# Weights of one expert tile issued earlier, two kinds of items moved between slots, and q's columns put in another order, in a two-layer transformer kernel

## Chip, cores and metric

The kernel runs on one core of one Trainium2 chip. The metric is the device time of one execution in microseconds (us), as the median of several runs. Five engines work on their own queues in program order: TensorE (PE in the profile), VectorE (DVE), ScalarE (ACT), GpSimd (POOL) and SyncE (SP), which here only issues DMAs. They hand work to each other over semaphores.

## What is computed

Input are 8 sequences of 256 tokens with 256 features. Two layers follow each other. Layer 0 is an attention with 16 heads and rotary parts, gated by a feed-forward block. Layer 1, which the change touches, is this:

```python
x = x + attention(xn) * silu(moe(xn))          # xn = layernorm(x)

# attention: 16 heads of 16 features, 256 tokens, 8 batches
q, k, v = split(xn @ w_qkv.T)
q = rmsnorm(q, q_norm_w); k = rmsnorm(k, k_norm_w)      # over the 16 features of a head
out = softmax(q @ k.T * 16 ** -0.5) @ v
out = out @ w_proj.T + b_proj

# moe: top 2 of 8 experts of width 176, and two shared ones
combine = normalised top-2 router probabilities
y = sum_e combine[:, e] * (silu(x @ gate[e]) * (x @ up[e])) @ down[e] + shared(x)
```

## The kernel before, in words

Products are made at high precision from two parts, a high one and a low one: `product` (lines 55 to 60) issues three matmuls, and every tile that feeds one is made in two steps, a copy by ScalarE (high part) and a subtraction by VectorE or GpSimd (low part).

Layer 1 is `stage_layer1`. Its time is cut into slots, `SLOTS` from -16 to 132. A slot n belongs to batch b = n // 16 and position u = n % 16, and in it TensorE makes the scores of head n + 1, then the items of the slot, then the transposes of the probabilities of head n - 1 (`turn`), then the values of head n - 2. There is one bank for scores and one for the transposed tile, so each waits until the other engines have read the one before. VectorE does in its slot the maximum of the scores of head n + 1 (L1699), the low part of the transposed tile of head n - 2 (L1703, named s_wh in the profile), some slot-bound work (the low part of an attention output in slots u = 2, 6, 10, 14, the sums of squares of q in u = 2 and of k in u = 3, the scaling in u = 7 and 8, row statistics in u = 14, the routing in three slots behind the router), then the first half of the slot's items, the reciprocal of the sum of the exponentials (L1730) and the second half of the items. ScalarE makes the exponentials (L1489) and the high parts, GpSimd the normalisation (L1374), the combine multiplication (L1381), the low part of the hidden values (L1385), and three rounds of a reciprocal root in u = 4, 5, 6.

The items of a slot come from `attn_jobs` (line 1095): Q0 and Q1 (projection of q and k for the next batch) at u = 0 and 1, V at 5, T (turn of the normalised rows) at 3, P0 and P1 (output projection of the batch before) at 3 and 4, X0 and X1 at `X_AT`: the turn of q and k of the first and second half of the heads. The router L and the turn of the combine weights C come once in two batches (a step s has 512 tokens). Between them a planner (lines 1117 to 1128) spreads the expert tiles: g, G, u, U are the four pieces of tile K (three matmuls over 512 columns each), D0 and D1 its down projection, taken two tiles later. It adds `SLOT_GOAL - UNIT` = 18.7 of credit a slot, takes off the costs of the items and fills in pieces, so moving an item moves pieces too. `halves` (line 1145) splits the items in two. A tile K belongs to step s = K // 14 with k = K % 14; the first three tiles of a step are the shared experts, the others take combine weights from DRAM.

SyncE's queue (lines 1245 to 1330) issues, tile by tile, the weights of the pieces (`load_gu`, 512 KB), of D (`load_d`, 256 KB), once a step the combine weights to DRAM (`store_combine`, which waits for its landing) and tile by tile back, spread over partitions (`load_cb`). In between, `stack_until` issues what the slots so far ask for: `store_stack` stores a turned half of q and k (X0 or X1) to DRAM, four stores, and `load_stack` loads two pairs of heads of it, four loads of q and one of k. The scores read the stacks.

In DRAM q lies as [half, parity, feature, low, pair, token], since its columns are ordered by `head_columns` as half, feature group, pair; parity is the head's place in its pair. So a load of q has runs of two pairs, and the sum over the 16 features of a head (`sum_squares`, L1625) reads with a step of 4 for q and 8 for k (`q = (4, 8)[r]`).

## Time and profile before

| | us |
|---|---|
| median of 3 runs | 1396.88 |
| lowest and highest | 1396.48, 1396.93 |
| the profiled execution | 1398.46 |
| its span, first to last instruction | 1396.7 |

| engine | busy us | share of the span |
|---|---|---|
| TensorE matmul | 1352.6 | 97% |
| TensorE weight load | 1205.1 | 86% |
| VectorE | 906.8 | 65% |
| ScalarE | 756.2 | 54% |
| GpSimd | 727.8 | 52% |

The profile is of one execution. Its times are those of that execution, with the span counted from the first instruction. Layer 1 begins at about 890 us. The mean granted clock of TensorE is 0.996 of full. Lines (L1699) are lines of the kernel file; names such as l_nb are the tiles' names with a prefix for the stage. In a timeline row, what stands in brackets is how long the engine was idle just before, and what ended that.

### The profile page before, as it was taken

Reading aid. Unit: us, or ns where it says so; the run is one execution under the profiler, and the core shown is the slowest. Engines: PE = TensorE matmul, PEld = TensorE weight load, DVE = VectorE, ACT = ScalarE, POOL = GpSimd, SP = SyncE. Lnnn points to the kernel's source line nnn. Section 1 sums busy time; section 2 is a strip of 40 time slices with the busy share of each in tenths; the row PEclk is TensorE's granted clock in tenths of the full one; section 3 lists DMA queues with packets and bytes.
Section 4 is the critical chain, followed back from the end, with each engine's and each line's share of the span. In section 5 each row is a group of like instructions: output and inputs, shape, how many; then the busy total and the mean of one; then the engine's idle time right before and its main releaser. Section 6 shows DMA issues by size and latency. Waiting matters only on the chain. (4 is left out here: it accounts for less than half of the span.)

```text
span 1396.7 us, 25325 instructions
## 1 busy us (share of the span) xinstructions
PE 1352.6 (97%) x8758; PEld 1205.1 (86%) x8758; DVE 906.8 (65%) x1807; ACT 756.2 (54%) x1964; POOL 727.8 (52%) x719
## 2 busy tenths in 40 slices
PE   8999899999999999999999999889999999999998
PEld 7887798999899989998998898768889888888897
DVE  6655566566656665666565665557887778786765
ACT  4553454445544555455545444246666666666664
POOL 1651343445343555344635453447657676766775
PEclk9999999999999999999999999999999999999999
DMA  5995333224422353234324424266555663645662
GB/s 185 318 337 202 84 91 97 84 77 120 113 82 49 103 144 85 62 91 114 97 63 120 118 63 127 95 189 186 162 169 156 197 176 112 205 138 181 177 194 91
DMA packets 105646, 190.51 MB, mean 136 GB/s; under 512 B 20433, under 2 KB 39569, under 8 KB 103217
## 3 DMA queue, kind: packets, MB, share of 16 engines
q1 hardware_dynamic: 105520, 188.91, 45.5%
q8 instruction: 71, 1.16, 0.4%
q14 instruction: 55, 0.44, 0.1%
HBM read 116.41 MB, written 30.47 MB: 105 GB/s over the span
## 5 line engine op out<-in xcount | busy, mean ns | idle before, releaser
L776 POOL TENSOR_TENSOR a_pr<-a_pr,a_ri 128x512 f32<-128x512 f32 x128 | 133.4, 1042 | 299.9 <-DVE a_ri L956 299.9
L833 ACT ACTIVATE a_pr<-a_score,a_nb 128x256 f32<-128x256 f32 x256 | 119.2, 471 | 267.7 <-DVE a_nb L948 267.7
L1374 POOL TENSOR_TENSOR l_pr<-l_pr,l_ri 128x512 f32<-128x512 f32 x128 | 133.3, 1042 | 126.4 <-DVE l_ri L1730 125.2
L1489 ACT ACTIVATE l_pr<-l_score,l_nb 128x256 f32<-128x256 f32 x256 | 119.3, 472 | 100.7 <-DVE l_nb L1699 100.7
L58 PE MATMUL a_job<-s_xs,s_wh 128*128 128x512 f32 x384 | 153.6, 400 | 1.0 <-PEq L222 1.0
L60 PE MATMUL a_job<-s_xs,s_wl 128*128 128x512 f32 x384 | 152.1, 396 | 0.0
L59 PE MATMUL a_job<-s_xs,s_wh 128*128 128x512 f32 x384 | 151.4, 394 | 0.0
L948 DVE TENSOR_REDUCE a_nb<-a_score 128x2 f32<-128x512 f32 x128 | 88.5, 692 | 86.1 <-PE a_score L1027 84.2
L1699 DVE TENSOR_REDUCE l_nb<-l_score 128x2 f32<-128x512 f32 x128 | 87.5, 684 | 32.1 <-PE l_score L1838 31.9
L961 DVE TENSOR_TENSOR a_pt<-a_turn,a_pt 128x512 fp32r<-128x512 f32 x128 | 87.5, 684 | 23.8 <-ACT a_pt L841 23.8
L58 PE MATMUL l_job<-l_xs,s_wl 128*128 128x512 f32 x224 | 90.3, 403 | 5.9 <-DMA s_wl<-wgu_scratch 5.8
L1497 ACT ACTIVATE s_wh<-l_turn 128x512 fp32r<-128x512 f32 x128 | 76.8, 600 | 35.4 <-PE l_turn L1848 35.4
L1703 DVE TENSOR_TENSOR s_wh<-l_turn,s_wh 128x512 fp32r<-128x512 f32 x128 | 87.3, 682 | 8.6 <-ACT s_wh L1497 8.2
L1862 PE MATMUL l_out<-s_wh,l_vp 128*128 128x256 f32 x512 | 91.9, 301 | 0.2 <-DVE s_wh L1703 0.2
L60 PE MATMUL l_job<-l_xs,s_wl 128*128 128x512 f32 x224 | 89.5, 399 | 0.0
L59 PE MATMUL l_job<-l_xs,s_wl 128*128 128x512 f32 x224 | 89.2, 398 | 0.0
L1848 PE MATMUL l_turn<-s_ident,l_pr 128*128 128x128 f32 x512 | 78.0, 275 | 11.3 <-DVE s_wh L1703 10.2
L956 DVE RECIPROCAL a_ri<-a_sm 128x2 f32<-128x2 f32 x128 | 21.3, 166 | 102.3 <-ACT a_pr L833 102.3
L60 PEld LDWEIGHTS a_job<-s_xs,s_wl 128*128 128x128 f32 x384 | 72.1, 188 | 16.8
L1848 PEld LDWEIGHTS l_turn<-s_ident,l_pr 128*128 128x128 f32 x512 | 58.7, 140 | 29.1 <-issue 12.8
L58 PEld LDWEIGHTS a_job<-s_xs,s_wh 128*128 128x128 f32 x384 | 72.3, 188 | 11.3 <-issue 1.4
L59 PEld LDWEIGHTS a_job<-s_xs,s_wh 128*128 128x128 f32 x384 | 72.3, 188 | 10.5
(252 smaller groups left out, 4565.4 us busy)
## 6 DMA issues: line engine op xcount, KB each, us to landing
s_wl<-wgu_scratch SPq DMA_DIRECT2D x56, 512.0 KB, 5.7
a_sk<-a_rotk SPq DMA_DIRECT2D x384, 64.0 KB, 2.0
a_sq<-a_rotq SPq DMA_DIRECT2D x256, 64.0 KB, 2.0
s_xs<-xn_scratch SPq DMA_DIRECT2D x14, 1024.0 KB, 5.6
l_wd<-wd_scratch SPq DMA_DIRECT2D x56, 256.0 KB, 2.9
l_zq<-qs_scratch SPq DMA_DIRECT2D x128, 64.0 KB, 4.3
l_sk<-ks_scratch SPq DMA_DIRECT2D x32, 256.0 KB, 4.7
a_raw<-in_w SPq DMA_DIRECT2D x30, 256.0 KB, 2.9
```

Source lines behind the costliest of these rows:

```text
L58: pe.matmul(out, lh, rh, start=first, stop=False)
L59: pe.matmul(out, lh, rl, start=False, stop=False)
L60: return pe.matmul(out, ll, rh, start=False, stop=last)
L776: pool.tensor_tensor(e, e, ri[:, n % 2, :].unsqueeze(2).broadcast_to([P, 2, SEQ]), ALU.mult)\
L833: i = act.activation(pr[:, n % 2, t, :], PS[n % 2][:, t * SEQ:(t + 1) * SEQ], ACT.Exp, bias=nb[:, n % 2, t:t + 1], accum_out=sm[:, n % 2, ...
L948: dve.tensor_reduce(nb[:, (n + 1) % 2, :], PS[(n + 1) % 2][:, :].rearrange("p (t k) -> p t k", t=2), AX.X, ALU.max, negate=True).then_inc( ...
L961: dve.tensor_tensor(pt[:, n % 2, 1, :], PT[:, :], pt[:, n % 2, 0, :], ALU.subtract).then_inc(S["turn_free"], 1)
L1374: pool.tensor_tensor(e, e, ri[:, n % 3, :].unsqueeze(2).broadcast_to([P, 2, SEQ]), ALU.mult)\
L1489: i = act.activation(pr[:, n % 3, t, :], PS[n % NPS][:, t * SEQ:(t + 1) * SEQ], ACT.Exp, bias=nb[:, n % 3, t:t + 1], accum_out=sm[:, n % 3 ...
L1699: dve.tensor_reduce(nb[:, (n + 1) % 3, :], PS[(n + 1) % NPS][:, :].rearrange("p (t k) -> p t k", t=2), AX.X, ALU.max, negate=True).then_in ...
L1848: i = pe.transpose(PT[:, kc * SEQ + t * P:kc * SEQ + (t + 1) * P], pr[:, n % 3, t, kc * P:(kc + 1) * P], ident[:, :])
L1862: i = pe.matmul(PO[:, 0:SEQ], vp[:, kc, a, e * P:(e + 1) * P], pt[:, n % 2, q, kc * SEQ:(kc + 1) * SEQ], start=(e == 0 and kc == 0 and q = ...
```

## The change

- `X_AT`: X1 of batches 1 to 7 comes in slot 13 instead of 10. X0, and batch 0, stay.
- P0 and P1 come in slots 4 and 5 instead of 3 and 4, but for the last batch's, which stay in slots 131 and 132.
- Only in step 0, `load_gu` of tile 5 (K = 4 is `first_combine`) is issued in front of the stack loads and the combine store asked for at K = 4, instead of at the start of K = 5.
- q's columns are ordered half, parity, pair, feature. The sum of squares of q reads with a step of 1; the scaling likewise. The DRAM copy is [half, parity, pair, feature, low, token], the stores and the four q loads of a stack follow, each partition now in two runs of 256 values instead of one of 512. `norm_w` is ordered for both. k's own order is as before.

The planner's result for three places, from working its sums through (items of a slot):

```
slot  before                          after
10    X1 D0 u U                       D0 u U D1
13    D1 g G                          X1 g G
19    T P0                            T D0 u
20    P1 l L                          U P0 l L
21    V                               V P1
22    D0 u                            (empty)
23    U D1 g                          D1 g
28    g G D0                          G D0 u
29    u U D1                          U X1 D1
35    T P0                            T g G
36    P1 g                            P0 D0
37    G V                             V P1
```

```diff
     def X_AT(m):
-        return (8, 9) if m == 0 else (9, 10)
+        return (8, 9) if m == 0 else (9, 13)
...
-        if u in (3, 4) and b >= 1:
-            jobs.append((f"P{u - 3}", b - 1))
+        first = 3 if b == BATCH else 4
+        if u in (first, first + 1) and b >= 1:
+            jobs.append((f"P{u - first}", b - 1))
...
-                        sp.dma_start(qs_dram[m % 2, half, :, :, low].rearrange("h d p n -> (h d) p n"), tqk[:, half, 0, low, :].bitcast(F32))                           .then_inc(tqk_out[half], 16)
+                        sp.dma_start(qs_dram[m % 2, half, :, :, :, low].rearrange("h p d n -> (h p d) n"), tqk[:, half, 0, low, :].bitcast(F32))                           .then_inc(tqk_out[half], 16)
...
-                        own = qs_dram[m % 2, half, h, :, :, j:j + PER_LOAD].rearrange("d c p n -> (d c) (p n)")
+                        own = qs_dram[m % 2, half, h, j:j + PER_LOAD].rearrange("p d c n -> (d c) p n")
                         for base in (64 * h, 64 * h + 32):
-                            sp.dma_start(zq[base:base + 32, h, at, :].bitcast(F32).rearrange("k p n -> k (p n)"), own)                               .then_inc(zq_in[stack_of(i)], 16)
+                            sp.dma_start(zq[base:base + 32, h, at, :].bitcast(F32), own)                               .then_inc(zq_in[stack_of(i)], 16)
...
                 for K in range(L + 1):
-                    if 2 <= K < L:
+                    s, k = step_of(K)
+                    first_combine = k == NSH + 1 and s == 0
+                    if 2 <= K < L and not (k == NSH + 2 and s == 0):
                         stack_until(AT["U", K - NGU] if K >= NGU else SLOTS[0])
                         load_gu(K)
                     if K >= 1:
                         stack_until(AT["D1", K - 1 - ND] if K > ND else SLOTS[0])
                         load_d(K - 1)
-                    s, k = step_of(K)
+                    if first_combine:
+                        load_gu(K + 1)
                     if k == NSH + 1 and s < NSTEP:
                         stack_until(AT["C", s])
                         store_combine(s)
...
                 def sum_squares(m, r):
-                    q = (4, 8)[r]
+                    q = (1, 8)[r]
...
                 def scale_rows(m, r):
-                    q = (4, 8)[r]
+                    q = (1, 8)[r]
...
-    qs = nc.dram_tensor("qs_scratch", [2, 2, 2, D1, 2, 4, SEQ], F32, kind="Internal").ap()
+    qs = nc.dram_tensor("qs_scratch", [2, 2, 2, 4, D1, 2, SEQ], F32, kind="Internal").ap()
...
-    return np.concatenate([q.transpose(0, 2, 3, 1, 4).reshape(D, D), k.transpose(0, 3, 1, 2, 4).reshape(D, D), w[2 * D:]])
+    return np.concatenate([q.transpose(0, 2, 1, 3, 4).reshape(D, D), k.transpose(0, 3, 1, 2, 4).reshape(D, D), w[2 * D:]])
...
-        "norm_w": _np.stack([_np.tile(_np.repeat(i[f"L1_attn_{s}_norm_w"], 4), 2) for s in "qk"], axis=1),
+        "norm_w": _np.stack([_np.tile(i[f"L1_attn_{s}_norm_w"], 8) for s in "qk"], axis=1),
```

## Rows read from the trace of the kernel before

**Rows 1.** Windows: stretch, length, busy us of each engine, clock, DMA share, GB/s.

```profile
400.00:700.00 300.00, 300.00 (x1950) 269.67 (x1949) 184.75 (x325) 154.67 (x395) 139.85 (x108) 1.00 0.34 95
...
1100.00:1200.00 100.00, 96.16 (x666) 86.48 (x665) 80.20 (x187) 68.77 (x198) 67.78 (x92) 1.00 0.53 158
```

**Rows 2.** Table of waits, TensorE, layer 1: in total, times, longest.

```profile
PE l_turn L1848 <- DVE s_wh L1703: 10.2, 26, 1.0
```

**Rows 3.** Timeline of TensorE, slot 115, which holds P0 and g: start, duration.

```profile
1338.13 0.40 PE L1838 MATMUL l_score<-l_sk,l_zq 128*128 128x256 f32 x2
1338.37 0.28 PE L58 MATMUL l_job<-s_wl,l_ot 128*128 128x256 f32 x1
...
1339.79 0.39 PE L58 MATMUL l_job<-l_xs,s_wl 128*128 128x512 f32 x1
...
1340.48 0.60 PE L1848 MATMUL l_turn<-s_ident,l_pr 128*128 128x128 f32 x4
...
1341.39 0.40 PE L1838 MATMUL l_score<-l_sk,l_zq 128*128 128x256 f32 x2
```

**Rows 4.** Timeline of TensorE: the scores with which slots 20, 21, 22 begin.

```profile
1002.96 0.40 PE L1838 MATMUL l_score<-l_sk,l_zq 128*128 128x256 f32 x2
...
1007.29 0.40 PE L1838 MATMUL l_score<-l_sk,l_zq 128*128 128x256 f32 x2
...
1010.09 0.39 PE L1838 MATMUL l_score<-l_sk,l_zq 128*128 128x256 f32 x2
```

**Rows 5.** Timeline, slot 42: scores, VectorE's maximum, the next scores.

```profile
1080.44 0.40 PE L1838 MATMUL l_score<-l_sk,l_zq 128*128 128x256 f32 x2
...
1082.49 0.68 DVE L1699 TENSOR_REDUCE l_nb<-l_score 128x2 f32<-128x512 f32 x1
...
1084.85 0.39 PE L1838 MATMUL l_score<-l_sk,l_zq 128*128 128x256 f32 x2
```

**Rows 6.** Timeline of TensorE: slot -1's g5, scores of slots 0 and 126.

```profile
931.25 0.77 PE L58 MATMUL l_job<-l_xs,s_wl 128*128 128x512 f32 x1 [5.80 <-DMA s_wl<-wgu_scratch]
...
935.23 0.63 PE L1838 MATMUL l_score<-l_sk,l_zq 128*128 128x256 f32 x2
...
1374.67 0.40 PE L1838 MATMUL l_score<-l_sk,l_zq 128*128 128x256 f32 x2
```

**Rows 7.** Windows, columns as in rows 1: the stretch behind the stall.

```profile
930.00:935.00 5.00, 3.75 (x11) 3.21 (x12) 0.18 (x1) 2.36 (x7) 3.99 (x6) 0.50 1.06 302
```

**Rows 8.** Timeline of GpSimd around the stall.

```profile
929.52 1.26 POOL L1381 TENSOR_TENSOR l_ga<-l_ga,l_cb 128x512 f32<-128x512 f32 x1 [10.15 <-DMA l_cb<-ct_scratch]
931.52 1.28 POOL L1385 TENSOR_TENSOR l_hid<-l_ga,l_hid 128x512 fp32r<-128x512 f32 x1 [0.74 <-ACT l_hid L1512]
```

**Rows 9.** Timeline of SyncE's queue: combine store, combine load, weights of tile 5.

```profile
922.27 0.54 SPq L1259 DMA_DIRECT2D ct_scratch<-l_ct  x1
924.54 0.36 SPq L1268 DMA_DIRECT2D l_cb<-ct_scratch  x1
924.94 0.43 SPq L1248 DMA_DIRECT2D s_wl<-wgu_scratch  x1
```

**Rows 10.** DMA issues of 256 KB of combine weights; q loads and q stores, ns on SyncE.

```profile
l_cb<-ct_scratch SPq DMA_DIRECT2D x16, 256.0 KB, 4.2
...
L1289 SPq DMA_DIRECT2D l_zq<-qs_scratch x128: 332/422/2137, 919.8 to 1352.2; - x128
...
L1274 SPq DMA_DIRECT2D qs_scratch<-l_tqk x32: 517/602/650, 914.0 to 1312.2; - x32
```

**Rows 11.** Instructions of L1625, eight for q and eight for k: ns min/median/max.

```profile
L1625 DVE TENSOR_REDUCE l_ss<-l_sqr x16: 1048/1104/1172, 899.2 to 1283.1; 128x32 f32<-128x512 f32 x16
```

**Rows 12.** Groups of instructions from 890 us: the maximum of the scores.

```profile
L1699 DVE TENSOR_REDUCE l_nb<-l_score 128x2 f32<-128x512 f32 x128 | 87.5, 684 | 32.1 <-PE l_score L1838 31.9
```

**Rows 13.** Timeline of VectorE, slot 41: the low part of X0.

```profile
1080.33 0.49 DVE L1577 SCALAR_TENSOR_TENSOR l_tqk<-l_job,s_nqk,l_tqk 128x256 fp32r<-128x256 f32 x1 [1.13 <-ACT l_tqk L1461]
```

**Rows 14.** Timeline of TensorE, slot 28: D0 of tile 14.

```profile
1034.47 0.36 PE L1758 MATMUL l_down<-l_wd,l_hid 128*128 128x256 f32 x1 [0.69 <-DVE l_y L1681]
```

## The prediction

> **What bounds the kernel now.** The page's first part gives the first reading: TensorE is busy for 97% of the span, VectorE for 65%. The windows of layer 0 show TensorE full from 400 to 700 us and nearly so before; nothing of the change lies there, so its time stays. In layer 1 TensorE is busy for 96 us of 100 [rows 1]. There the table of waits is read next: from 925 us on TensorE waits 26 times, 10.2 us in all, in its transposes of the probabilities on VectorE [rows 2], once for 5.8 us on the weights of tile 5, and twice on the bias sum of a finished step.
>
> The timeline of one full slot gives the prices of TensorE's work [rows 3]: from start to start the scores take 0.24 us, a projection (12 products) 1.42, a piece of an expert tile 0.69, transposes and values 0.91. A slot without items is thus 1.15 us of work; D0 or D1 is 0.71 (six products of 0.118), Q and V cost as much as P, T, X and C 0.35 each, and the router 1.76 (slot 20, with P1, lasts 4.33 [rows 4]). With W as a slot's sum, a slot that nothing holds up lasts W: this one holds 1.15 + 1.42 + 0.69 = 3.26 and lasts 3.26.
>
> The timeline of slot 42 shows what holds one up [rows 5]. Its scores start at 1080.44, but VectorE, late from slot 41, takes their maximum at 1082.49: a lag of 2.05. Then come its low part of the turned tile, the transposes that wait for it, values, and the next scores at 1084.85, which is 2.36 us behind the maximum. So a slot lasts max(W, lag + 2.36), and an entirely empty one, with the smallest lag of 0.43, 2.79: slot 21, W 2.57, lasts 1010.09 - 1007.29 = 2.80 with a lag of 0.43 [rows 4]. I read the lag of all 127 slots this way from the same two timelines; the rule gives the length within 0.03 us in over twenty of the held-up ones. From slot 0 to the end of slot 125 (935.23 to 1374.67 us [rows 6]) 439.4 us pass and the W sum to 414.8. These 24.6 us, and the stall before slot 0, are all that a new order of the same work can win.
>
> **Early weights.** The stall looks like 5.8 us plus a half clock: TensorE stops at 925.4, resumes at 931.25 [rows 6], and from 930 to 935 the granted clock is 0.50, its 1.2 GHz level, at which half of the time is lost [rows 7]; it is back at 936.2. With g5 and G5 at the slow pace that is some 8 us. But behind G5 in slot -1 stands D0 of tile 3, and it needs that tile's hidden values, which are late themselves: GpSimd waited 10.15 us for the combine weights, multiplied at 929.52, ScalarE copied, and GpSimd subtracted at 931.52 for 1.28 us [rows 8]. So D0 could start at 932.80 at the soonest against 933.95, where it started. And that chain hangs on SP's queue: eight stores of the turned halves from 914.02 on, wd, the first stack, then the combine store at 922.27, its landing, and the combine load at 924.54; the weights of tile 5 are issued behind it, at 924.94 [rows 9]. The change puts them (0.43 us of SP) in front of the stack, the combine store and the load. Combine load, then D0, move later by 0.43, and by up to four times 0.18 more if the q loads, which become three-dimensional, take SP as long as the stores do (0.60 for 0.42 us). The load's 4.8 us to landing may fall to 4.2, the median for its size, without 512 KB right behind it [rows 10]. D0 then starts at 932.6 to 933.95, TensorE having stood still since some 927. At half pace it takes 1.28 us, so the next scores start at 933.9 to 935.2 against 935.23: 0 to 1.3 us won. The clock came back 5 us after TensorE resumed; if it does so again, it is back at 937.6 or later where it was back at 936.2, and slots 0 and 1 have 2.7 us more of slow time, half of it lost: 1.35. Net between 1.35 lost and 0.05 lost; up to 3.4 won (2.9 on the scores and the 0.5 that slot 0 lost to the slow clock) if the shorter stop does not drop the clock. I take 0.3 lost: slots 0 and 1 hang in part on VectorE, which the slow clock does not touch. Stack 0 gets 512 KB ahead of it and may hold the first scores for up to 1 us, which the later wait for D0 hides.
>
> **q by parity, pair, feature.** The sum of squares of q reads with a step of 4 values, that of k of 8: the 16 of them take 1.05 to 1.17 us, those of q the lower end [rows 11]. Step 1 is nearest to the maximum over 512 values, 0.684 [rows 12]. So 0 to 0.38 us of VectorE a batch; I take 0.38, in slot 2 of each batch, so the lag at slot 3 is smaller. The scaling makes the same 512 results. The q loads fetch two runs of 1 KB for one of 2 KB in each partition; the stores write 1 KB runs already, and in all of layer 1 the scores waited once, for 0.2 us, on a stack: nothing, up to 1 us lost.
>
> The Trainium skill, "SBUF — State Buffer", "Door 1: The DMA port swizzle", has 16-byte lines and calls a step of 4 fp32 free. By it the new order wins nothing and the sum is 2.0 us longer; the 1.05 us beside 0.684 speaks against that, though the second reads PSUM, so it is rival (e).
>
> **Second half's turn at slot 13.** Nothing goes; X1 moves. A slot with an X costs VectorE 1.13 us of waiting for ScalarE's two copies [rows 13] and 0.8 of its own, 4.0 to 4.6 us in all for W 2.9, so the next begins with a lag of 1.5 to 2.05 and lasts 0.6 to 1.2 over W. In the kernel before the second X follows at once and drags the lag over slots 10 to 12. After the change slot 10 has time to catch up, and slot 14 pays a second time. The planner's sum, worked through with the new items, puts four pieces in some slots 10, 11 and 12. Over W in slots 9 to 16, before and after by the rule: batch 0 1.5 and 1.0; 2 2.5 and 2.9; 3 0.6 and 0.4; 4 2.1 and 1.8; 5 1.9 and 0.65; 6 2.8 and 2.5. Batch 1 has 3.2 and 3.6: there X1 meets the gate of step 0 (two operations over 512 values) in slot 29, and D0 of tile 14 comes behind one piece where it came behind two, so its 0.69 us wait for the bias sum [rows 14] becomes 1.4. Sum 14.6 to 12.85: 1.75 us won. Bounds: if each X slot costs as slot 41 did, 2 lost; if ScalarE is free sooner in slot 13, 5 won. SP issues the four stores of X1 four slots later; the stack that needs them is asked for only in slot 4 of the next batch, so this costs nothing; it would if that queue ran three slots late.
>
> **Projections in slots 4 and 5.** Batches 1, 3 and 5 (slots 20, 52, 84) have the router there. The planner now fills slot 19 with a D0 and a piece, slot 20 with U, P0 and the router (W 5.0), slot 21 with V and P1 (3.99), and leaves slot 22 empty. The empty slot still lasts 2.79: 1.6 over W, and slot 23, W 2.54, another 0.45 since the routing on VectorE leaves a lag of 0.63. Before, slots 19 to 23 were 1.24, 1.29 and 1.50 over W; after 2.1 each. In batches 2, 4 and 6 P0 leaves the slot with the second sum of squares and the xs split, but G comes there: 0.72, 0.9, 0.5 before, 0.86, 1.05, 0.45 after. Batch 0 wins 0.4 from the shorter sum alone. Sum 6.6 to 8.7: 2.1 us lost, with the 0.38s of q inside. Bounds: 5 lost if GpSimd (three rounds of the root, a spread and a normalise in slots 20 to 22) is late too; 1 won if the lags are as small as in batch 7. The last projections stay in slots 131 and 132, and the end is unchanged.
>
> **The sum.** -0.3 + 1.75 - 2.1 = -0.65 won, so 0.6 us longer: a span of 1396.7 becomes 1397.3, and the profiled execution's 1398.46 becomes 1399.1. It lies 1.6 above the median of the three runs, 1396.88, so against that I forecast 1397.5.
>
> **Rivals.**
> (a) No change within 0.2% (2.8 us, about what a measurement of this kernel can tell from none), as summed: 0.41.
> (b) Clock kept and lags small: the stop before slot 0 is short enough for the full clock, 3.4 won, and slots 9 to 16 win 3 while slots 22, 54 and 86 cost 1.5 in all: 1396.9 - 4.9 = 1392. For it: TensorE would stand still for some 5 us instead of 5.8. Against: in those 5.8 us the level fell [rows 7]. Chance 0.27.
> (c) The weights were all of the stall, because the combine load lands far sooner without them behind it: D0 at 932 or before, 4.5 to 8 won, 1390. Against: 256 KB of combine weights take 4.2 us as the median, too. Chance 0.04.
> (d) Slower by the empty slots 22, 54 and 86. It decides from the point where slots 19 to 21 give nothing back: 1.64 + 0.44 each, 6.2 in all, and X1 beside the row statistics of slot 14 loses the 2 of its bound, while the shorter sums win 3.5: 4.7 longer, 1401.6. Chance 0.2.
> (e) The order of q does not do what it says: the sum stays at 1.05 us. Slot 3 then starts with a lag 0.38 larger and lasts some 0.29 longer in seven batches: 2.0, so 1399.5. Chance 0.08.
> Faster by over 0.2% are (b) and (c), 0.31; the same (a) and nearly all of (e), 0.48; slower (d) and the rest, 0.21. The range 1391 to 1401.5 leaves out half of (c) and of (d); for the likeliest alone it is 1394.5 to 1399.6.
>
> **What would show it.** L1625 for q at 0.69; the wait on the weights gone and TensorE waiting some 5 us on GpSimd's hidden values in slot -1 in its place; the combine load issued at 925 or later; slots 22, 54 and 86 lasting 2.8; a 1.4 us wait on the bias sum in slot 28; lags of 1.5 to 2 at slots 10 and 14. I am wrong if D0 of tile 3 starts before 932, if the clock stays full through 930 to 940, or if slot 14 begins with a lag below 1.

## The result, and the profile after

The changed kernel takes 1399.9 us (median of 20 runs, 1397.52 to 1402.98), the kernel before 1397.43 (median of 20, 1395.72 to 1402.71). The ratio is 1.0018, with a 95% interval from 1.0011 to 1.0024: 2.5 us slower, inside the 0.2% that I had called no change, and four times the 0.6 us of my sum. The profiled execution of the changed kernel has a span of 1399.9 us and a time of 1401.74.

The page of the changed kernel, first the busy time of each engine, then the transfers, then two groups of instructions and one of DMA issues:

```profile
PE 1353.7 (97%) x8758; PEld 1208.1 (86%) x8758; DVE 908.7 (65%) x1807; ACT 757.3 (54%) x1964; POOL 725.0 (52%) x719
...
DMA packets 109741, 190.51 MB, mean 136 GB/s; under 512 B 20432, under 2 KB 47760, under 8 KB 107312
...
L1703 DVE TENSOR_REDUCE l_nb<-l_score 128x2 f32<-128x512 f32 x128 | 87.6, 684 | 39.0 <-PE l_score L1842 38.5
...
L1852 PE MATMUL l_turn<-s_ident,l_pr 128*128 128x128 f32 x512 | 77.9, 274 | 15.5 <-DVE s_wh L1707 15.2
...
l_zq<-qs_scratch SPq DMA_DIRECT2D x128, 64.0 KB, 4.6
```

The engines' lines of layer 1 stand 4 further down than in the kernel before, SyncE's 1. The row that matters is that of the transposes of the probabilities: TensorE waited 10.2 us there before [rows 2] and waits 15.2 now. VectorE itself has longer pauses for want of scores, 39.0 us where it had 32.1 [rows 12]. The two engines' busy time grows by only 1.1 and 1.9 us; they wait for each other more often. The loads of q, now in two runs a partition, land after 4.6 us in the median (4.3 before), and TensorE never waits for one in layer 1 of this execution.

I split the span by the instants at which slots begin (the scores in TensorE's timeline), and take each slot's own work off its length, by the prices of the prediction:

| part, profiled executions, us | before | after | difference |
|---|---|---|---|
| start of the span to the first TensorE instruction of layer 1 | 891.80 | 894.20 | +2.40 |
| from there to the scores of slot 0 | 43.43 | 41.35 | -2.08 |
| slots 0 to 125 | 439.44 | 442.43 | +2.99 |
| scores of slot 126 to the end of VectorE's last instruction | 19.40 | 19.39 | 0 |
| over W: slots 0 to 2 of the batches | 1.72 | 2.03 | +0.31 |
| slots 3 to 7 | 7.25 | 12.20 | +4.95 |
| slot 8 | 1.82 | 1.24 | -0.58 |
| slots 9 to 16 | 14.53 | 12.78 | -1.75 |

Slot 16 of a batch is slot 0 of the next, so it stands in two rows (0.72 us before, 0.66 after); slots 9 to 15 alone are 13.81 and 12.12.

The 2.40 us of the first row are none of the change: its code for layer 0 is the same, and over the kernels below this stretch lasts 889.4 to 893.5 us with no relation to what they change. Part of it can be seen. In this execution TensorE waited 2.79 us for a load at 142 us, and its granted clock then fell to 1.2 GHz for part of the window from 145 us, and once more in that from 165 us, so that its mean in both is 0.66 of full; in the execution of the kernel before it is 1.00 in both. Windows with their columns as in [rows 1]:

```profile
145.00:150.00 5.00, 5.00 (x21) 4.30 (x21) 1.00 (x3) 1.62 (x5) 1.04 (x1) 0.66 0.43 105
...
165.00:170.00 5.00, 4.31 (x17) 3.81 (x18) 2.63 (x5) 1.86 (x6) 0.73 (x2) 0.66 0.38 90
```

Of the fourteen executions only e9_x_by_batch also has such stretches in layer 0, and these two begin layer 1 last, at 894.20 and 893.53. Layer 1 itself became 0.91 us longer in this pair of executions.

**Before slot 0.** The timelines of TensorE (first row), GpSimd (two) and SyncE's queue (three), and the windows with their columns as in [rows 1]:

```profile
934.11 0.58 PE L1762 MATMUL l_down<-l_wd,l_hid 128*128 128x256 f32 x1 [4.48 <-POOL l_hid L1389]
...
930.79 1.26 POOL L1385 TENSOR_TENSOR l_ga<-l_ga,l_cb 128x512 f32<-128x512 f32 x1 [9.01 <-DMA l_cb<-ct_scratch]
932.79 1.27 POOL L1389 TENSOR_TENSOR l_hid<-l_ga,l_hid 128x512 fp32r<-128x512 f32 x1 [0.74 <-ACT l_hid L1516]
...
921.65 0.45 SPq L1249 DMA_DIRECT2D s_wl<-wgu_scratch  x1
924.64 0.54 SPq L1260 DMA_DIRECT2D ct_scratch<-l_ct  x1
927.28 0.35 SPq L1269 DMA_DIRECT2D l_cb<-ct_scratch  x1
...
930.00:935.00 5.00, 0.89 (x4) 0.89 (x5) 0.76 (x2) 2.03 (x6) 3.48 (x3) 0.90 0.97 303
935.00:937.00 2.00, 2.00 (x9) 1.81 (x9) 0.78 (x2) 0.69 (x2) 2.00 (x5) 0.50 1.04 297
```

The weights are issued three microseconds ahead of the combine store, and the 5.80 us wait for them [rows 6] is gone. In its place D0 of tile 3 waits 4.48 us for its hidden values, and the chain behind that is the one of [rows 8, 9], one for one: GpSimd waits 9.01 us for the combine weights, multiplies, ScalarE copies, GpSimd subtracts. One thing differs from what I had: the combine load lands 3.51 us after its issue (927.28 to GpSimd's start at 930.79), where it took 4.98 before. And the clock falls to 1.2 GHz only from 934.0 and is full again at 937.4, 3.3 us after TensorE resumed; before, it was down from 929.5 to 936.3, until 5 us after TensorE resumed.

**Slots 21 to 23**, one of the three places where the planner leaves a slot empty. TensorE's timeline:

```profile
1011.90 0.39 PE L1842 MATMUL l_score<-l_sk,l_zq 128*128 128x256 f32 x2
1013.80 0.63 PE L1852 MATMUL l_turn<-s_ident,l_pr 128*128 128x128 f32 x4 [1.51 <-DVE s_wh L1707]
1014.74 0.40 PE L1842 MATMUL l_score<-l_sk,l_zq 128*128 128x256 f32 x2
1017.18 0.63 PE L1852 MATMUL l_turn<-s_ident,l_pr 128*128 128x128 f32 x4 [0.64 <-DVE s_wh L1707]
1018.12 0.39 PE L1842 MATMUL l_score<-l_sk,l_zq 128*128 128x256 f32 x2
```

The empty slot 22 lasts 2.84 us for 1.15 of work, with a wait of 1.51; slot 23 lasts 3.38 for 2.54. Slots 54 and 55 last 3.04 and 3.38, slots 86 and 87 2.90 and 3.38. VectorE (five rows) and GpSimd (two) over the same time:

```profile
1007.80 1.12 DVE L1598 TENSOR_TENSOR l_lg<-l_lg,l_m 128x32 f32<-128x32 f32 x1
...
1012.38 0.68 DVE L1703 TENSOR_REDUCE l_nb<-l_score 128x2 f32<-128x512 f32 x1
...
1014.11 0.49 DVE L1663 TENSOR_TENSOR l_eq<-l_eq,l_m 128x32 f32<-128x32 f32 x1
...
1015.33 0.32 DVE L1667 TENSOR_TENSOR l_oh<-l_oh 128x32 f32<-128x32 f32 x1
...
1015.77 0.67 DVE L1703 TENSOR_REDUCE l_nb<-l_score 128x2 f32<-128x512 f32 x1
...
1007.57 1.30 POOL L1385 TENSOR_TENSOR l_ga<-l_ga,l_cb 128x512 f32<-128x512 f32 x1
...
1013.28 1.27 POOL L1389 TENSOR_TENSOR l_hid<-l_ga,l_hid 128x512 fp32r<-128x512 f32 x1
```

From maximum to maximum VectorE's slot 22 takes 3.39 us; I had its routing at the length that it had before (2.99), which would have made the lag at slot 23 0.63. It is 1.03. The instruction at 1014.11 has only 32 values a partition, yet it ends when GpSimd's subtraction over 512 ends (1014.60 and 1014.55), and the one at 1007.80 ends with GpSimd's multiplication (1008.92 and 1008.87). In the kernel before, the same two, in VectorE's timeline:

```profile
1007.16 0.59 DVE L1594 TENSOR_TENSOR l_lg<-l_lg,l_m 128x32 f32<-128x32 f32 x1
...
1012.66 0.24 DVE L1659 TENSOR_TENSOR l_eq<-l_eq,l_m 128x32 f32<-128x32 f32 x1
```

Here the moved pieces of the expert tiles bring GpSimd's long operations beside the routing. The long one, at 1007.80, costs TensorE nothing, since slot 21 has 3.99 us of work of its own; the quarter of a microsecond at 1014.11 and the 0.12 at 1015.33 (0.32 us for 0.20) stand in the slot that has nothing to hide them, and are most of the 0.40.

The other traces bear this out. Over all fourteen, 34 of the routing's VectorE instructions with two inputs in SBUF began within a GpSimd operation of over 1 us that had at least 0.25 us to go: every one ended 0.04 to 0.06 us behind it and took 0.42 to 1.15 us. The 43 beside one that have a single SBUF input (the copy, the reductions, the addition from the matmul's bank l_job) took 0.17 to 0.19. The 60 instructions of the three routings of slots 0 to 125 take 12.25 us before, 11.9 to 12.3 in the kernels below that leave the projections of the router's batches in slots 3 and 4, 15.65 in the changed kernel, 15.64 in e10 and e12 and 14.37 in e1; the time by which the overlapped ones exceed 0.19 us makes 0.40 us of it before and 3.39 after. The Trainium skill, "SBUF — State Buffer", "SBUF: two separate sides", has VectorE operations with two SBUF inputs and GpSimd's share one pair of ports that one of them holds for a whole instruction; these ends agree with it. No kernel here takes the overlap away alone.

**q's order.** VectorE's sixteen sums of squares, min/median/max in ns:

```profile
L1629 DVE TENSOR_REDUCE l_ss<-l_sqr x16: 671/872/1167, 901.5 to 1285.5; 128x32 f32<-128x512 f32 x16
```

Against 1048/1104/1172 before [rows 11]. The eight of q take 0.67 to 0.68 us (0.68 at 901.54), the eight of k 1.07 to 1.17 (1.11 to 1.17 before).

### The profile page after: what moved, and what is told of

It is laid out like the page before. It is cut to its first block and busy times, and to the rows that moved or that the text cites. A ratio compares the mean times of both kernels' runs of the same rounds, so it can differ in the third digit from the quotient of the medians.

```text
span 1399.9 us, 25325 instructions
## 1 busy us (share of the span) xinstructions
PE 1353.7 (97%) x8758; PEld 1208.1 (86%) x8758; DVE 908.7 (65%) x1807; ACT 757.3 (54%) x1964; POOL 725.0 (52%) x719
## 5 line engine op out<-in xcount | busy, mean ns | idle before, releaser
L1852 PE MATMUL l_turn<-s_ident,l_pr 128*128 128x128 f32 x512 | 77.9, 274 | 15.5 <-DVE s_wh L1707 15.2
```

The costliest lines, as they stand in the source:

```text
L1852: i = pe.transpose(PT[:, kc * SEQ + t * P:kc * SEQ + (t + 1) * P], pr[:, n % 3, t, kc * P:(kc + 1) * P], ident[:, :])
```

## The experiments

Twelve kernels, each timed against the kernel before on its own chip; there the kernel before had medians of 1398.11 us (e1 to e4), 1397.18 (e5 to e8) and 1396.67 (e9 to e12), so it is the ratios that compare. "Slots" is the length of slots 0 to 125 in the profiled execution, "to slot 3" the time from layer 1's first TensorE instruction to the scores of slot 3 (it takes in the stall and the slow clock behind it), "turn" TensorE's wait for VectorE in the transposes from the page:

| kernel | ratio, 95% interval | median, us | to slot 3 | slots | turn |
|---|---|---|---|---|---|
| before | 1 | 1397.43 | 52.47 | 439.44 | 10.2 |
| after | 1.0018, 1.0011 to 1.0024 | 1399.90 | 50.80 | 442.43 | 15.2 |
| e1_p_only | 1.0042, 1.0030 to 1.0054 | 1404.06 | 52.26 | 446.59 | 18.2 |
| e2_x_only | 0.9979, 0.9968 to 0.9990 | 1395.10 | 51.45 | 437.25 | 7.3 |
| e3_weights_only | 0.9993, 0.9985 to 1.0002 | 1396.80 | 51.15 | 441.01 | 10.2 |
| e4_q_only | 0.9973, 0.9963 to 0.9983 | 1394.26 | 51.77 | 437.03 | 7.5 |
| e5_no_p | 0.9960, 0.9946 to 0.9975 | 1391.58 | 51.35 | 436.46 | 7.5 |
| e6_p_even | 0.9978, 0.9967 to 0.9989 | 1394.34 | 53.72 | 437.38 | 9.9 |
| e7_store_first | 0.9948, 0.9932 to 0.9964 | 1390.43 | 50.86 | 436.65 | 7.5 |
| e8_best | 0.9938, 0.9922 to 0.9953 | 1388.76 | 48.87 | 436.26 | 7.3 |
| e9_x_by_batch | 0.9962, 0.9947 to 0.9976 | 1392.48 | 51.83 | 436.61 | 6.8 |
| e10_after_store_first | 0.9991, 0.9982 to 1.0000 | 1396.09 | 48.82 | 442.55 | 14.8 |
| e11_q_and_x | 0.9958, 0.9944 to 0.9973 | 1391.60 | 51.08 | 435.03 | 7.7 |
| e12_p_odd | 0.9999, 0.9989 to 1.0009 | 1396.51 | 51.07 | 440.83 | 13.1 |

A difference between two kernels is taken between the ratios, 0.001 being 1.4 us, and has an error of some 2 us; where the timelines say the same, I trust it more. The timelines are of one execution each. How well their sums repeat is seen in e3, whose edit ends before slot 0: its slots are 1.57 us longer, 0.33 of it in slot 0 and the rest in slots 14 to 95. Slot 70 alone takes part in many of these differences, since TensorE waits at its end up to 1.1 us for a stack in some executions (0.16 before, 1.09 in e5) and not at all in others (the changed kernel).

### The four parts alone

The kernel before with the projections' move alone:

```diff
-        if u in (3, 4) and b >= 1:
-            jobs.append((f"P{u - 3}", b - 1))
+        first = 3 if b == BATCH else 4
+        if u in (first, first + 1) and b >= 1:
+            jobs.append((f"P{u - first}", b - 1))
```

> The kernel before with P0 and P1 in slots 4 and 5 alone. Theory S (slots): the cost of this edit in the changed kernel was 4.9 us in slots 3 to 7 of the batches (7.25 us over W before, 12.2 after), and here the sum of squares of q is not shorter, so 5 to 6.5 us longer than before; slots 22, 54 and 86, empty, last 2.8 to 3.3 and slots 23, 55, 87 3.4 (W 2.55). Theory E (elsewhere): what the changed kernel lost does not sit in these slots but was there already at the start of layer 1, which came 2.4 us later in its profiled execution; then this kernel is within 1.5 us of before.

Measured: 5.9 us slower, within theory S's bounds, and theory E falls. Slots 3 to 7 of the batches are 13.27 us over W where they were 7.25, the three pairs of empty slots and their successors last 2.87/3.38, 2.80/3.32 and 2.83/3.39, and TensorE's wait in the transposes is the largest of all kernels. The group of the page:

```profile
L1849 PE MATMUL l_turn<-s_ident,l_pr 128*128 128x128 f32 x512 | 78.1, 275 | 18.3 <-DVE s_wh L1704 18.2
```

The second half's turn at slot 13 alone:

```diff
-        return (8, 9) if m == 0 else (9, 10)
+        return (8, 9) if m == 0 else (9, 13)
```

> The kernel before with X1 in slot 13 alone. Theory S: slots 9 to 16 of all batches were 14.5 us over W before and 12.8 after the whole change, slot 8 of batch 4 another 0.5 less: 1.7 to 2.2 us faster than before, batch 5 winning most (1.45) and batch 2 losing 0.7. Theory E: no part of it is worth more than 1 us, the time is that of before within 1 us.

Measured: 3.0 us faster, above the expectation, whose value the interval (1.4 to 4.5 us) holds. The slots are 2.19 shorter, and the wait in the transposes falls from 10.2 to 7.3. Theory E falls.

The early weights alone:

```diff
-                    if 2 <= K < L:
+                    s, k = step_of(K)
+                    first_combine = k == NSH + 1 and s == 0
+                    if 2 <= K < L and not (k == NSH + 2 and s == 0):
...
-                    s, k = step_of(K)
+                    if first_combine:
+                        load_gu(K + 1)
```

> The kernel before with the weights of tile 5 issued ahead of the first stack alone. Theory S: from the first instruction of layer 1 on TensorE to the scores of slot 0 took 43.4 us before and 41.4 after, and slot 0 was 0.4 longer: 1.5 to 2 us faster; TensorE waits 4 to 5 us for GpSimd's hidden values in front of D0 of tile 3, and the combine load lands 3.5 us after its issue, since no 512 KB are queued right behind it (4.8 before). Rival theory: those 3.5 us were chance and it lands after 4.8 here too; then D0 starts as late as before and nothing is won (0 to 0.5).

Measured: 1.0 us faster by the ratio, with no change inside the interval: less than theory S's 1.5 to 2, though its steps hold. TensorE's D0, GpSimd's multiplication and the issue of the combine load in the three timelines:

```profile
930.61 0.58 PE L1761 MATMUL l_down<-l_wd,l_hid 128*128 128x256 f32 x1 [4.54 <-POOL l_hid L1388]
...
927.29 1.26 POOL L1384 TENSOR_TENSOR l_ga<-l_ga,l_cb 128x512 f32<-128x512 f32 x1 [9.40 <-DMA l_cb<-ct_scratch]
...
923.83 0.35 SPq L1268 DMA_DIRECT2D l_cb<-ct_scratch  x1
```

Again the load is there after 3.46 us. So the shorter landing is no accident of one execution; with the weights right behind the load it takes 4.4 to 5.0 (before, e1, e2, e4, e11), with them in front 3.5 to 3.6 (after, e3, e5, e9, e12), with one execution at 4.6 (e6). The three kernels with the store first, below, have the weights in front too and land at 3.9 to 5.2, so the weights' place is not all of it.

The order of q alone (the same lines as in the change):

```diff
-                    q = (4, 8)[r]
+                    q = (1, 8)[r]
```

> The kernel before with q's columns by parity, pair, feature alone. Theory S: the sum of squares of q falls from 1.06 to 0.68 us in each batch, slot 3 starts with a lag 0.38 smaller where it is not waiting for ScalarE, and lasts up to 0.3 less in six batches: 0.5 to 2 us faster. Theory E: the two runs of 1 KB in place of one of 2 KB in each partition, or the place of the data in DRAM, cost time somewhere: 1 to 2.5 us slower.

Measured: 3.8 us faster, twice the upper end of what was expected; theory E falls. The slots are 2.41 shorter, at the lower end of what the ratio's interval allows (2.4 to 5.2); the rest of the 3.8 is not in them and may be the spread of the medians. With X1 at slot 13 in both kernels the order gives nearly the same in the slots (2.22, e11 against e2), and so does X1 with the new order in both (2.00, e11 against e4). The sixteen sums of squares are 14.5 us in all instead of 17.6, which is 8 times 0.38.

### Without the projections' move, and where its loss lies

The changed kernel with P0 and P1 back in slots 3 and 4:

```diff
-        first = 3 if b == BATCH else 4
-        if u in (first, first + 1) and b >= 1:
-            jobs.append((f"P{u - first}", b - 1))
+        if u in (3, 4) and b >= 1:
+            jobs.append((f"P{u - 3}", b - 1))
```

> The changed kernel with P0 and P1 back in slots 3 and 4. Theory S (the prices of the slots add up): the changed kernel is 2.5 us slower than before and the projections cost it 4.9, so this one is 2 to 3.5 us faster than before. Theory E (the loss is not in these slots): it stays 1.5 to 2.5 us slower than before.

Measured: 0.9960, faster than the kernel before by 5.6 us and than the changed one by 0.58% or some 8 us, of which 5.97 stand in the slots. More than theory S's 2 to 3.5; theory E falls. Its row of the transposes:

```profile
L1851 PE MATMUL l_turn<-s_ident,l_pr 128*128 128x128 f32 x512 | 77.7, 274 | 8.2 <-DVE s_wh L1706 7.5
```

The move in the batches without the router, and then in those with it (the last batch has neither loss nor gain, 0.02 and 0.03 us over W):

```diff
-        first = 3 if b == BATCH else 4
+        first = 4 if b % 2 == 0 and b < BATCH else 3
```

> The changed kernel with P0 and P1 back in slots 3 and 4 in batches 1, 3, 5 and 7 alone; in 2, 4 and 6 they stay in 4 and 5. Theory S: the empty slots beside the router are the loss, 4.2 us of 4.9 in batches 1, 3 and 5; without them this kernel is 1.2 to 2.5 us faster than before. Rival: the projection itself is badly placed in slots 4 and 5 wherever it stands (the G beside the second sum of squares); then only some 2 of the 4.9 come back and this kernel is about as fast as before.

Measured: 0.9978, 3.1 us faster than before, more than theory S's 1.2 to 2.5; the rival, no gain over before, falls. Against e5_no_p the slots are only 0.92 longer, but this execution's D0 waited 5.86 us before slot 0, where others with early weights waited 4.5 to 5.0. Its granted clock was at 1.2 GHz from 899.7 to 906.6 us, where it did not fall in e5_no_p, and the combine store behind that came 2.0 us later after layer 1's start (32.1 against 30.1). So most of its 2.5 us over e5_no_p is not shown to be the projections'.

```diff
-        first = 3 if b == BATCH else 4
+        first = 4 if b % 2 == 1 and b < BATCH else 3
```

> The changed kernel with P0 and P1 in slots 4 and 5 only in batches 1, 3, 5 and 7 (the router's batches and the last), the complement of e6_p_even. Theory R (the empty slots 22, 54 and 86 are most of the loss): slots 3 to 7 at 10.5 to 11.5 us over W, of which batches 1, 3 and 5 some 2.7 each, and 4.0 to 5.5 us over e5_no_p: ratio 0.999 to 1.000. Rival A (both kinds of batch cost alike): 2.5 to 3 us over e5, ratio 0.998. By TensorE's slots alone, which give the even batches only 0.9, it is R with 4.5 us: 0.9992.

Measured: 0.9999, theory R. It costs 0.39% or 5.4 us over e5_no_p, 4.37 of them in the slots; batches 1, 3 and 5 are 2.59, 2.80 and 2.64 us over W in slots 3 to 7 (0.99, 1.11 and 1.23 in e5_no_p), the others as without the move. The group of the page:

```profile
L1852 PE MATMUL l_turn<-s_ident,l_pr 128*128 128x128 f32 x512 | 77.7, 274 | 13.2 <-DVE s_wh L1707 13.1
```

In the slots the two sets of batches make 4.4 and 0.9 of the 5.97; the 0.7 that is left is within what such sums vary by.

### The early weights beside the others

The changed kernel with neither the projections' move nor the early weights (only the lines of q and of slot 13):

```diff
-                    if 2 <= K < L and not (k == NSH + 2 and s == 0):
+                    if 2 <= K < L:
...
-                    if first_combine:
-                        load_gu(K + 1)
```

> The order of q and X1 at slot 13, without the early weights and without the move of the projections. Theory W (the early weights are worth 1 to 2 us beside the others too): 1 to 2 us over e5_no_p, a ratio of 0.9967 to 0.9975, slot 0 reached 42.3 to 43.0 us after layer 1's start, the combine load landing 4.4 to 5.0 us after its issue. Rival Z (the landing time was chance): 0.996 as e5, slot 0 at 41.1, landing at 3.5.

Measured: 0.9958 against the 0.9960 of e5_no_p. Of theory W the mechanism holds (slot 0 is reached after 42.03 us instead of 41.11, the load lands in 4.43) and the price does not: nothing is left of it. Where it goes is seen in slot 0. TensorE's timeline and windows of 1 us of e5_no_p, with early weights:

```profile
929.97 0.58 PE L1761 MATMUL l_down<-l_wd,l_hid 128*128 128x256 f32 x1 [4.79 <-POOL l_hid L1388]
...
931.42 0.63 PE L1841 MATMUL l_score<-l_sk,l_zq 128*128 128x256 f32 x2
...
935.67 0.40 PE L1841 MATMUL l_score<-l_sk,l_zq 128*128 128x256 f32 x2
...
931.42:932.42 1.00, 1.00 (x5) 0.90 (x5) 0.34 (x1) 0.39 (x1) 1.00 (x3) 0.50 1.05 252
...
934.42:935.42 1.00, 1.00 (x4) 0.81 (x3) 0.90 (x5) 0.78 (x2) 0.12 (x1) 0.50 0.83 187
935.42:936.42 1.00, 1.00 (x7) 0.83 (x6) 0.70 (x3) 0.31 (x1) 0.54 (x1) 0.89 0.14 45
```

and of e11_q_and_x, without them:

```profile
929.00 0.77 PE L58 MATMUL l_job<-l_xs,s_wl 128*128 128x512 f32 x1 [4.74 <-DMA s_wl<-wgu_scratch]
...
932.97 0.63 PE L1838 MATMUL l_score<-l_sk,l_zq 128*128 128x256 f32 x2
...
935.60 0.39 PE L1838 MATMUL l_score<-l_sk,l_zq 128*128 128x256 f32 x2
...
932.97:933.97 1.00, 1.00 (x5) 0.92 (x5) 0.69 (x3) 0.08 (x1) 0.90 (x2) 0.67 1.02 290
```

In e5_no_p all of slot 0 runs at 1.2 GHz: 4.25 us from scores to scores, and the clock is back 5.7 us after TensorE resumed. In e11_q_and_x TensorE resumed earlier, with slot -1's g5, G5 and D0 still ahead of it (3.97 us at the slow clock), the clock is back 4.6 us after it resumed, and most of slot 0 is at full speed: 2.63 us. The 0.92 us won ahead of slot 0 are lost in it, and 0.7 more. But this is a reading of two executions, and the slow stretch is not the same from one to the next. In the windows of the fourteen, the clock fell at the stop before slot 0 in all but e8; in three (after, e3, e10) it was down half as long as in the ten others, partly while TensorE still stood, and it was full again 3.2 to 6.2 us after TensorE resumed. The changed kernel has the same early weights and gives back only 0.37 us in slot 0 (3.18 against 2.81). That nothing is left of the weights' gain rests on the medians, with their error of some 2 us.

### The combine store ahead of the queue

e5_no_p with the first combine store ahead of wd and of the stack, its landing awaited behind the stack:

```diff
+                    if first_combine:
+                        stack_until(AT["D1", K - 1 - ND])
+                        wait_free(sp, ("C", 0))
+                        sp.dma_start(ct_dram[0], ct[:, :]).then_inc(ct_stored[0], 16)
                     if K >= 1:
                         stack_until(AT["D1", K - 1 - ND] if K > ND else SLOTS[0])
                         load_d(K - 1)
                     if first_combine:
                         load_gu(K + 1)
-                    if k == NSH + 1 and s < NSTEP:
+                        stack_until(AT["C", s])
+                        sp.wait_ge(ct_stored[0], 16)
+                    elif k == NSH + 1 and s < NSTEP:
```

> The changed kernel without the move of the projections, and with the first combine store issued in front of wd of tile 3 and of stack 0, its landing awaited behind the stack. Theory S (SP's queue sets the stall): the combine load is issued some 2.2 us sooner than in the changed kernel, TensorE waits 2 to 2.5 us instead of 4.5 in slot -1, the clock stays full, and the kernel is 2 to 3 us faster than the one without the move of the projections, 4 to 6 faster than before. Rival: the hidden values of tile 3 come as late as before for another reason (the load lands later for the traffic of the stack in front of it); then it is within 0.7 us of the kernel without the move.

Measured: 0.9948, 1.7 us under e5_no_p by the ratio (1.2 by the medians), a little under what was expected. GpSimd's multiplication and SyncE's issue of the combine load:

```profile
925.43 1.26 POOL L1390 TENSOR_TENSOR l_ga<-l_ga,l_cb 128x512 f32<-128x512 f32 x1 [8.36 <-DMA l_cb<-ct_scratch]
...
920.28 0.59 SPq L1268 DMA_DIRECT2D l_cb<-ct_scratch  x1
```

Both the theory and the rival are right in part. Counted from layer 1's start, the load is issued 2.3 us sooner than in e5_no_p, but it lands 5.15 us after its issue where it took 3.58, so D0 comes only 0.75 us sooner. The stop (TensorE's wait for the hidden values in front of D0) is 3.52 us and not 2 to 2.5, and the clock does fall: TensorE resumed at 928.75 and had the slow clock until 934.96, another 6.2 us, so slot 0 lasts 4.27 us again.

The same on top of the whole change:

> The changed kernel, all four parts, with the first combine store ahead of wd and the stack. Theory S: the store wins what it won in e7 (1.2 us of the median), the stall in slot -1 is 3.5 instead of 4.5 us, slots 3 to 7 are still 12 to 13 us over W: ratio 1.0009, span some 1 us under that of the changed kernel. Rival H (the projections' loss is really a loss of the stall, so a cure of the stall cures it): slots 3 to 7 fall with it, ratio under 0.998.

Measured: 0.9991, 3.8 us under the changed kernel. TensorE's D0, GpSimd's multiplication, and SyncE's store and load:

```profile
927.29 0.39 PE L1768 MATMUL l_down<-l_wd,l_hid 128*128 128x256 f32 x1 [2.75 <-POOL l_hid L1395]
...
923.96 1.28 POOL L1391 TENSOR_TENSOR l_ga<-l_ga,l_cb 128x512 f32<-128x512 f32 x1 [7.36 <-DMA l_cb<-ct_scratch]
...
915.86 0.54 SPq L1327 DMA_DIRECT2D ct_scratch<-l_ct  x1
...
919.79 0.59 SPq L1269 DMA_DIRECT2D l_cb<-ct_scratch  x1
```

The gain is more than theory S's 1.2 us, and its steps hold: the stop shrinks to 2.75 us, slot 3 is reached 2.0 us sooner than in the changed kernel, and slots 3 to 7 stay at 12.44 over W, so the projections' loss is theirs and rival H falls. The group of the transposes has hardly moved:

```profile
L1858 PE MATMUL l_turn<-s_ident,l_pr 128*128 128x128 f32 x512 | 77.8, 274 | 15.0 <-DVE s_wh L1713 14.8
```

The store is also all that sets e8_best below apart from e9_x_by_batch. The three pairs (e7 against e5, e10 against after, e8 against e9) put its worth at 1.7, 3.8 and 3.4 us by the ratios, and at 0.5, 2.0 and 3.0 by the time to slot 3: more than the weights gave in all but the first of the timelines, and spread as the load's landing is (5.15, 4.17 and 3.87 us).

### Slot 13 by batch, and the best version

e7_store_first with X1 at slot 10 again for m of 2, 3 and 4, which are the batches 1 to 3 in which the changed kernel was not shorter in slots 9 to 16:

```diff
-        return (8, 9) if m == 0 else (9, 13)
+        return (8, 9) if m == 0 else (9, 10) if m in (2, 3, 4) else (9, 13)
```

> The kernel with the first combine store in front, and X1 in slot 13 only for batches 1, 5, 6 and 7, in slot 10 for 2, 3 and 4. Theory S: by the slots, X1 at 13 lost 0.7, 0.2 and 0.1 us in those three batches; so 0.5 to 1 us faster than with X1 at 13 in all batches. Rival: the batches influence each other through the lag at their borders and nothing is won or some tenths are lost.

Measured: 0.9938, interval 0.9922 to 0.9953: the fastest of all, 8.4 us under the kernel before on its chip. But its slots are only 0.39 us shorter than e7_store_first's. The rest lies before slot 3 (48.87 against 50.86). D0 waits 2.31 us, and this is the one execution whose clock does not fall behind that stop; TensorE's timeline and one window behind it:

```profile
928.33 0.38 PE L1767 MATMUL l_down<-l_wd,l_hid 128*128 128x256 f32 x1 [2.31 <-POOL l_hid L1394]
...
928.00:929.00 1.00, 0.67 (x5) 0.67 (x6) 0.62 (x2) 0.33 (x1) 1.00 (x2) 1.00 1.05 281
```

Even so the full clock gives little in slots 0 and 1: they last 2.33 and 4.43 us, since TensorE then waits 1.50 us for ScalarE's exponentials, against 4.27 and 2.90 in e7.

The choice by batch on e5_no_p, without the early store, tells the two apart:

> The changed kernel without the move of the projections (e5_no_p), and X1 at slot 13 only for batches 1, 5, 6 and 7's halves, at slot 10 for those of 2, 3 and 4. e8_best beat e7_store_first by 1.7 us of the median with this same edit, but its trace shows only 0.4 us less in slots 0 to 125 and 1.6 less in the stall before slot 0. Theory B (the choice itself matters): 0.4 to 1.0 us under e5_no_p, that is a ratio of 0.9953 to 0.9957 against e5's 0.996, slots 9 to 15 at 11.0 to 11.5 us over W. Rival N (e8's lead was the stall's own variation from execution to execution): 0.996 again, and stalls before slot 0 that differ by up to 1.5 us between kernels that issue the same instructions there.

Measured: 0.9962 to e5_no_p's 0.9960, slots 436.61 to 436.46. Theory B falls: the choice by batch is worth nothing that the slots show, and rival N stands. In the profiled pair e8's lead over e7 is the stretch before slot 0, where both issue the same instructions and the combine load landed after 3.87 us instead of 5.15. That their six runs each differ by 1.7 us in the median for the same reason is argued from this pair and not shown. e7_store_first is as good a version as can be shown, 0.5% faster than the kernel before; e8_best has the lowest median.

## Why the prediction came out as it did

The forecast was no change within 0.2%, 0.6 us longer by the sum and 1397.5 us against the three runs shown. Measured: 1399.9, 2.5 us longer, in the range. The sign of the sum was right and its size a quarter of the measured one. That it came so near is partly luck, since two terms were off in opposite ways: in the pair of profiles the projections cost 2.85 us more than their term, and the stretch up to slot 3, put at 0.3 lost, won 1.67.

**Bound and rule.** TensorE's slots and the lag of VectorE were the right view: what grew between the two pages is the transposes' wait. With the lags of the trace after, the rule max(W, lag + 2.36) gives 4.06 for slot 36 (lag 1.70; it lasts 4.07), 4.59 for slot 42 (lag 2.23; 4.60) and 4.42 for slot 100 (lag 2.06; 4.43). The empty slots begin with lags of 0.48, 0.68 and 0.54, not the least lag of 0.43, and last what the rule makes of that: 2.84, 3.04 and 2.90. Of the 43 slots of the kernel before that VectorE holds up, the rule gives 38 within 0.03 us.

**Early weights: -0.3, the steps right, their balance wrong.** D0 follows GpSimd's hidden values, with a wait of 4.48 us that I had at some 5. D0 came 2.24 us sooner counted from layer 1's start, more than the 1.35 I allowed: the combine load landed in 3.5 us, where I had 4.2 to 4.8, and the q loads took SyncE no longer, 1.84 us for four. In the profiled execution 1.67 us are won by slot 3. But over all kernels, those with the early weights reach slot 3 after 51.24 us on average (five, without e6_p_even; 51.65 with it) and those without after 51.81 (five): 0.2 to 0.6 won, and by the ratios 1.0 alone and none beside q and slot 13. So the price that I put on the clock, 1.35 us given back in slots 0 and 1, is there in some executions (slot 0 at 4.25 in e5 against 2.63 in e11) and small in others (3.18 in the changed kernel against 2.81 before); I was wrong in letting it outweigh the gain. One of the three signs of being wrong did come: D0 before 932. It stands at 934.11 only because layer 0 took 2.40 us longer; counted from layer 1's start it is where 931.7 was in the kernel before. And the 3.4 us that a kept clock was to win do not come out of the prediction's own rows: D0 at 932.6 and 0.64 us for it put the scores at 933.2, 2.0 sooner, which with slot 0's 0.5 is 2.5.

**q's order: right, and perhaps too small.** L1629 is 0.68 for q, as taken; rival (e) falls. I put some 2 us on it. The slots gave 2.4 alone (e4 against before) and 2.2 beside slot 13 (e11 against e2); the ratios say 3.8 and 2.9. By place it came otherwise: I had 0.29 us in slot 3 of seven batches, and in e4 slot 3 is shorter by 0.15 us or more in batches 1, 2 and 6 only, and slot 4 in 2, 4 and 5. By the rule of the Trainium skill, "SBUF — State Buffer", "Door 1: The DMA port swizzle", that a step of 4 fp32 is free, nothing would have been won: the measured 1.05 against 0.68 us decides against it.

**Second half's turn: right in the sum.** 1.75 forecast and 1.75 measured in slots 9 to 16 of the pair (14.53 to 12.78), with lags of 1.68 and 1.50 at slots 10 and 14 of batch 0. Batch by batch it holds less well: batch 1, put at 0.4 lost, lost 0.1, batch 2, put at 0.4 lost, lost 0.7, and batches 0 and 5 won more than forecast. A second sign of being wrong came here: slot 14 begins with a lag below 1 in batches 3, 4 and 5 (0.93, 0.80, 0.54), so the turn in slot 13 does not delay VectorE everywhere as slot 41 had it. The bias sum's wait for D0 of tile 14 became 1.37, forecast 1.4, in TensorE's timeline:

```profile
1035.23 0.35 PE L1762 MATMUL l_down<-l_wd,l_hid 128*128 128x256 f32 x1 [1.37 <-DVE l_y L1685]
```

Alone (e2) it gave 3.0 us.

**Projections: the step that was mis-sized.** "Sum 6.6 to 8.7: 2.1 us lost" was 7.25 to 12.20, 4.95 lost, in the pair; taken apart from q, 4.1 had been forecast (the 2.1 and q's 2.0) and 5.9 to 7.2 in the slots, 6 to 8 by the ratios, was measured (e1 against before, after against e5, e10 against e7). By place: batches 1, 3 and 5, forecast 2.1 each, are 2.59, 2.80 and 2.66. Two thirds of the excess is in slots 23, 55 and 87, which are 0.83 over W where I had 0.45. That was the step "since the routing on VectorE leaves a lag of 0.63"; it is 1.03. I carried over the length the routing had, without asking what GpSimd does beside it after the pieces have moved. Another 0.4 us in all is the empty slots' own lag. Batch 6, forecast 0.45, is 2.07. Of this 0.92 is slot 103's wait for the bias sum, which is there before as well (0.91) and which I left out of both sums: the batch had 1.34 before, not 0.5. The other 1.15 is slot 100, in which VectorE is late from slot 99, where its operation for G waits 0.62 us for ScalarE's tanh (a lag of 2.06, 4.43 us long for 3.28); this I did not work out. Batch 0 was to win 0.4 from the shorter sum and won nothing, because VectorE then waited 0.40 us for ScalarE instead. In batch 2 the forecast holds (0.86; 0.90), in batch 4 it was too high (1.05; 0.62). The lower bound that I gave, 5 lost "if GpSimd is late too", was the nearest to it.

**The rivals.** (b) does not happen in this change: the clock fell all the same. It is real, though, in e8_best, with a stop of 2.31 us. (c) had its true half in the landing time, worth a microsecond and not four. (d) is the one that came nearest in its mechanism, with the empty slots and their successors as its place, at 7.8 us over W for its 6.2; its other half, X1 losing 2 us, is refuted by e2.

**What stays open.** The parts alone sum to 0.13% faster by their ratios, the whole is 0.18% slower. By the slots they sum to 4.1 us longer (7.15 - 2.19 + 1.57 - 2.41) and the whole is 2.99 longer. The intervals of five ratios together are wide enough for the first (each some 0.1% to either side); I don't read an interaction into it. Of the 2.5 us by which the medians of before and after differ, the pair of profiles shows 0.9 in layer 1; the rest is not located, and the slow clock's stretches, which came in other places and lengths in each execution, are as large as that. Why they came where they did is open. That GpSimd's long operations stretch the routing is read from the rows of fourteen traces and was not tried by itself; what it costs TensorE, some 0.4 us in each of slots 23, 55 and 87, is worked out by the rule of the lags. Why the combine load lands after 3.9 to 5.2 us behind the early store is open too.

## To carry to other kernels

When an engine stands still behind a chain of transfers, shorten the chain: the weights that it waited for by name gave 0 to 1 us by the ratios, the store at the head of the next-latest chain 2 to 4. Where items of a plan are moved, work through every engine that shares a slot, GpSimd and ScalarE too, and not only the engine that paces; a slot left empty costs its full turn-around time (2.8 to 3.0 us here) and its neighbour pays again. And count what a stop costs at the slow clock on the work that follows it, since that can take back all that a shorter stop wins, as in e5 against e11. One profile of each kernel does not show a difference of 2 us: compare the stretches that the edit touches, and look at the clock in those that it does not.

## What the runs showed of the hardware that I had not expected

- A VectorE sum of squares over 512 fp32 of SBUF takes 0.67 to 0.68 us with a step of 1, 1.05 to 1.10 with a step of 4, which is 16 bytes, and 1.11 to 1.17 with 8. Steps of 2 and 3 were not run.
- A 256 KB load that is issued with 512 KB right behind it lands 4.4 to 5.0 us after its issue, and with that 512 KB in front of it after 3.5 to 3.6 (once 4.6). With the store moved ahead as well, so that the load comes 2.3 to 2.7 us sooner, it took 3.9, 4.2 and 5.2.
- At the stop before slot 0 the granted clock fell to 1.2 GHz in thirteen executions whose work there is nearly the same, between 3.3 us before and 0.4 us after TensorE resumed, and was full again 3.2 to 6.2 us after it resumed. Those thirteen stops lasted 2.75 to 5.86 us; a stop of 2.31 us left the clock at 2.4 GHz, and one of 2.79 us in layer 0 did not.
- A VectorE operation over 32 values with two inputs in SBUF took 1.12 us, ending with GpSimd's 1.3 us operation that began before it, where it takes 0.2 alone; 34 of 34 such overlaps ended that way. This instruction's four instances in the changed kernel, min/median/max, were `311/974/1124` ns against `192/317/589` before.
